# Mixture-of-experts FFN: transposes of h by VectorE squares and quadrant transfers, down projection two blocks behind, weight loads of experts 1 to 7 issued by GpSimd

## Chip, core and metric

One core of one Trainium2 chip runs the kernel. The metric is the device time in microseconds of one execution, as the median of repeated runs. Beside it stands one profiled execution, from which every row in this document comes.

## What is computed

Tokens x are (4, 512, 256). A first layer adds a normalised and projected x together with a decayed running sum over context rows that is gathered by patch index. The second layer, which the change concerns, is a mixture of experts: 2,048 tokens, 8 experts, the two best per token, width 256 to 1024 to 256, all in float32.

```python
x = x + xattn(layernorm(x), ctx_2048, mask, W_in, b_in, g_res, g_init)
z = layernorm(x)
probs = softmax(z @ gate_w)
w, idx = top_k(probs, 2); w = w / w.sum(-1, keepdims=True)
out = 0
for i in range(8):
    wi = where(idx == i, w, 0).sum(-1)
    h = silu(z @ w1[i]) * (z @ w3[i])       # 256 -> 1024
    out = out + (h @ w2[i]) * wi[..., None] # 1024 -> 256
x = x + out
```

## The kernel before

**Front part.** For some 114 us the kernel computes the first layer, the router, and lists that sort the tokens by expert into blocks of 128 token slots. At most 39 blocks can occur; here there are 37. A table in SBUF holds one word for each block: its expert, the expert of the block before, and flags that say which part of the next expert's weights is to be prepared in this step (F_CHUNK, F_W2, F_W3) and whether a further expert's weights are to be loaded (F_LOAD). Every engine reads this word and walks over the blocks in its own loop (`over_steps`, L289), two blocks per turn of the loop. What orders the engines among each other is semaphores alone; each engine works its own instructions in the order written.

**Precision.** A matrix product in float32 is made of three passes in the fast format (`three`, L1308): each operand is split into a high part (a ScalarE copy into float32r) and a low part (a VectorE subtraction), and hi*hi, hi*lo and lo*hi are accumulated. This holds for the weights (`split_hi` L313, `split_lo` L318, 2,048 columns a chunk, three chunks per expert) and for each transposed activation (`xT`, `hT`).

**One block.** GpSimd gathers 128 rows of z from DRAM (`block_rows`, L473). TensorE transposes them (L1319), ScalarE and VectorE split the result into xT_hi and xT_lo. TensorE makes gate and linear part for 512 of the 1024 hidden columns at a time (`up`, L1322, 12 matmuls of 512 columns for each of two halves); ScalarE does silu (L612), VectorE the product with the linear part, hmul (L1091). TensorE transposes hmul, four squares of 128x128 for each half (`hT`, L1331), into one PSUM bank per half. ScalarE copies it to hT_hi (L607), VectorE subtracts to get hT_lo (L1099). TensorE then does the down projection (`down`, L1338, 24 matmuls of 256 columns), ScalarE scales by the routing weight (`y`, L617) and GpSimd adds the rows to the output in DRAM by an indirect transfer (`add_rows`, L481), which waits until the add before it has landed.

**Order on TensorE in step i (L1353).** up half 0 of block i; transposes of h half 1 of block i-1; transposes of x of block i+1; up half 1; transposes of h half 0 of block i; down of block i-1. So the down projection is one block behind. `drain` (L1371) finishes the last block.

**Weights.** SyncE issues all of them (`raw_load`, L263: three transfers of 1 MB an expert; w1 and w3 have rows of 4 KB, w2 of 1 KB). Experts 0 and 1 are loaded in the front part, expert 2 once expert 0 is split, and expert e+3 in the step in which the last chunk of expert e+1 is split (L386 on). GpSimd splits the low parts of expert 0 itself (L461 to L471). In its steps SyncE does nothing else.

Of the kernel before, what the change touches and what calls it, by code (L numbers as in the profile page):

```python
# [22 lines left out]
P = 128  # L23
# [3 lines left out]
T = B * S  # L27
# [12 lines left out]
TABLE = 1 + 2 * STEP_PAIRS + 3  # L40
# [4 lines left out]
OUT_INIT = 32  # L45
# [6 lines left out]
def build(nc, x, ctx, lens, w_in, b_in, g_res, g_init, gate_w, w1, w3, w2, out):  # L52
# [12 lines left out]
    with stack:  # L65
# [111 lines left out]
        with ExitStack() as early:  # L177
# [9 lines left out]
        dg = sb("dg", [P, 2, TPB, D], f32)  # L187
# [59 lines left out]
            hT0hi_ready hT0lo_ready hT1hi_ready hT1lo_ready xT_done xThi_ready xTlo_ready  # L247
# [7 lines left out]
        blk_in = [sem(f"blk_in{q}") for q in range(2)]  # L255

# [32 lines left out]
        def over_steps(eng, body):  # L289

            body(0, 0, 0, step_word(eng, 0))
            with eng.Fori(0, STEP_PAIRS) as pair:
                word = step_word(eng, pair * 2 + 1)
                with eng.If(word & F_RUN):
                    body(pair * 2 + 1, 1, pair, word)
                    word = step_word(eng, pair * 2 + 2)
                    with eng.If(word & F_RUN):
                        body(pair * 2 + 2, 0, pair + 1, word)

        def block_count(eng):  # L300
            eng.wait_ge(s["blocks_ready"], 1)
            return eng.value_load(blocks_i[:, :], min_val=E, max_val=BLOCKS)

        def at_end(eng, blocks, drain):

            with eng.If(blocks & 1):
                drain(blocks - 1, 0)
            with eng.If((blocks + 1) & 1):
                drain(blocks - 1, 1)
# [17 lines left out]
        def _(sp):  # L327
# [31 lines left out]
            parts = [(e, m) for e in range(2) for m in range(3)]  # L359
            for k in range(B + 2):  # L360
# [17 lines left out]
                for e, m in parts[max(k - 1, 0):k] if k < B + 1 else parts[k - 1:]:  # L378
                    raw_load(sp, e, e, s["raw_ready"] if e else s["raw_first"], (m,))


            sp.wait_ge(s["lo_first"], 3)
            sp.wait_ge(s["raw_ready"], RAW_SEM)
            sp.wait_ge(s["xT_done"], 1)
            raw_load(sp, 2, 0, s["raw_ready"])
            sp.wait_ge(s["table_ready"], 1)  # L386

            def step(i, q, half, word):
                with sp.If(word & F_LOAD):
                    e = expert(word).with_bounds(min_val=0, max_val=E - 4)  # L390
                    sp.wait_ge(s["lo_ready"], e * 3 + 6)
                    settle(sp)
                    sp.wait_ge(s["raw_ready"], RAW_SEM * (e + 2))
                    settle(sp)
# [1008 lines left out]
```

## Time and profile before

| | us |
|---|---|
| median of 3 runs | 495.22 |
| fastest run | 494.84 |
| span of the profiled execution (first to last instruction) | 492.8 |
| TensorE busy in it | 422.1 |
| VectorE busy | 263.6 |
| ScalarE busy | 192.5 |
| GpSimd busy | 169.9 |

Busy time is the time in which the engine works on at least one instruction; matmuls overlap each other and the weight loads (PEld), so a busy TensorE may still be able to be fuller. PEclk or granted clock is the share of TensorE's full 2.4 GHz that it was given; 0.5 is 1.2 GHz. SyncE (SP) has no compute; its rows are the issues of transfers, and "to landing" is the time from an issue to the completion of its data. The name behind "<-" in brackets is what ended the idle time before an instruction.

### The profile page before, as it was taken

What the parts mean: (1) busy time and instruction counts of PE and PEld (TensorE: products, weight loads), DVE (VectorE), ACT (ScalarE), POOL (GpSimd) and SP (SyncE); (2) the same over time, 40 slices, a digit from 0 to 9 for tenths busy, and PEclk for the clock granted to TensorE, in tenths of its full rate; (3) what the DMA queues carried; (4) which work ended last, traced back from release to release, by engine and by line L of the source; (5) the groups of instructions that cost most, each with busy time, mean ns of one, the idle gap of its engine ahead of it and who ended that gap; (6) DMA issues with size and microseconds to landing.
All of it is one profiled execution on the core that took longest, in us unless ns stands there. A gap on an engine that the chain in (4) does not pass through costs nothing.

```text
span 492.8 us, 10407 instructions
## 1 busy us (share of the span) xinstructions
PE 422.1 (86%) x2557; PEld 365.9 (74%) x2558; DVE 263.6 (53%) x670; ACT 192.5 (39%) x334; POOL 169.9 (34%) x133
## 2 busy tenths in 40 slices
PE   0678984314999999999999999999999999999980
PEld 0556864313888889888888988888898888889870
DVE  7877869997454255433563564355356433653230
ACT  3446443301444246233542643354264334542230
POOL 5455434442023333322242333224233322532321
PEclk9979795555999999999999999999999999999995
DMA  6856885604415421541118118111811211121120
GB/s 196 297 179 206 272 268 157 200 1 139 161 23 160 149 32 32 203 105 23 30 21 287 32 21 283 32 26 21 287 32 21 32 30 23 21 32 32 21 32 11
DMA packets 33076, 50.92 MB, mean 103 GB/s; under 512 B 3335, under 2 KB 25095, under 8 KB 33063
## 3 DMA queue, kind: packets, MB, share of 16 engines
q1 hardware_dynamic: 24983, 38.44, 23.4%
q0 software_dynamic: 8080, 12.33, 12.8%
q8 instruction: 5, 0.08, 0.1%
q14 instruction: 8, 0.07, 0.0%
HBM read 39.36 MB, written 11.40 MB: 103 GB/s over the span
## 4 chain that ended last, share of the span: by engine, by line
PE 73%; DVE 7%; issue 2%; DMA 1%; POOL 1%; ACT 1%; ACTq 0%; POOLq 0%; DVEq 0%
PE bank L1312 64%; PE bank L1335 7%; PE bank L1319 2%; DVE ctx_sb L901 2%; DVE onehot_lo L986 1%; DVE rank L889 1%; DMA dg<-depool_rows,plugi 1%; PE bank L1266 1%; POOL dg L441 1%; DMA xblk<-z_rows,gidx 1%; PE bank L1191 0%; DVE batch L990 0%; POOL out L485 0%; DVE st L823 0%; DVE x_all L820 0%
## 5 line engine op out<-in xcount | busy, mean ns | idle before, releaser
L1312 PE MATMUL bank<-split,xT_hi 128*128 x592 | 166.8, 403 | 1.3 <-DVE xT_lo L1087 1.3
L1096 DVE TENSOR_TENSOR hmul<-gact,bank 128x512 f32<-128x512 f32 x74 | 50.9, 688 | 149.1 <-ACT gact L614 149.1
L485 POOL DMA_INDIRECT out<-yblk,itok x37 | 78.4, 2118 | 149.8 <-ACT yblk L621 138.2
L1312 PEld LDWEIGHTS bank<-split,xT_hi 128*128 128x128 f32 x592 | 106.9, 190 | 22.6 <-issue 1.9
L1312 PE MATMUL bank<-split,hT 128*128 (+1 forms) x888 | 115.4, 286 | 1.4 <-issue 0.8
L1312 PEld LDWEIGHTS bank<-split,hT 128*128 128x128 f32 x888 | 108.5, 191 | 2.1 <-issue 1.2
L614 ACT ACTIVATE gact<-bank 128x512 f32<-128x512 f32 x74 | 44.2, 598 | 158.9 <-PE bank L1312 158.8
L1312 PE MATMUL bank<-split,xT_lo 128*128 x296 | 93.7, 398 | 0.0
L477 POOL DMA_INDIRECT xblk<-z_rows,gidx x40 | 40.1, 1001 | 106.0 <-DVE gidx L1109 100.3
L321 DVE TENSOR_TENSOR split<-raw,split x21 | 48.1, 2293 | 37.6 <-ACT split L315 37.6
L1312 PEld LDWEIGHTS bank<-split,xT_lo 128*128 128x128 f32 x296 | 56.0, 189 | 13.5
L1102 DVE TENSOR_TENSOR hT<-bank,hT 128x512 fp32r<-128x512 f32 x74 | 50.6, 684 | 3.7 <-ACT hT L609 3.7
L315 ACT ACTIVATE split<-raw (+1 forms) x24 | 45.9, 1912 | 2.8 <-issue 1.9
L1335 PEld LDWEIGHTS bank<-ident,hmul 128*128 128x128 f32 x296 | 36.9, 141 | 10.3 <-DVE hmul L1096 0.4
L1335 PE MATMUL bank<-ident,hmul 128*128 128x128 f32 x296 | 44.4, 272 | 0.0
L609 ACT ACTIVATE hT<-bank 128x512 fp32r<-128x512 f32 x74 | 43.9, 593 | 1.1 <-issue 1.0
L621 ACT ACTIVATE yblk<-bank,wtok 128x256 f32<-128x256 f32 x37 | 17.6, 475 | 47.5 <-PE bank L1312 35.7
L605 ACT ACTIVATE xT_hi<-bank 128x256 fp32r<-128x256 f32 x38 | 14.9, 392 | 21.2 <-PE bank L1319 21.2
L441 POOL DMA_INDIRECT dg<-depool_rows,plugi x16 | 15.5, 969 | 19.7 <-issue 12.1
L1087 DVE TENSOR_TENSOR xT_lo<-bank,xT_hi 128x256 fp32r<-128x256 f32 x38 | 15.8, 415 | 3.2 <-ACT xT_hi L605 3.2
L1245 PE MATMUL bank<-gate,batch 128*128 128x8 f32 x64 | 11.5, 317 | 6.8 <-DVE base L880 6.1
L1245 PEld LDWEIGHTS bank<-gate,batch 128*128 128x128 f32 x64 | 11.1, 270 | 7.6 <-DVE base L880 6.5
(182 smaller groups left out, 332.4 us busy)
## 6 DMA issues: line engine op xcount, KB each, us to landing
raw<-in_L_ffn_w SPq DMA_DIRECT2D x24, 1024.0 KB, 8.0
ctx_sb<-in_ctx SPq DMA_DIRECT2D x4, 1024.0 KB, 6.4
x_all<-in_x SPq DMA_DIRECT2D x4, 512.0 KB, 8.3
depool_rows<-gact SPq DMA_DIRECT2D x4, 512.0 KB, 3.0
out<-x_all SPq DMA_DIRECT2D x4, 512.0 KB, 5.5
z_rows<-z SPq DMA_DIRECT2D x4, 512.0 KB, 3.9
xblk<-z_rows,gidx POOLq DMA_INDIRECT x40, 2.8
out<-yblk,itok POOLq DMA_INDIRECT x37, 4.7
```

The costliest lines, as they stand in the source:

```text
L315: act.activation(split_chunk[:, ds(raw3 * 2 + m, 1)], raw_chunk[:, ds(raw3 + m, 1)], ACT.Copy)\
L321: dve.tensor_tensor(split_chunk[:, ds(raw3 * 2 + m + 3, 1)], raw_chunk[:, ds(raw3 + m, 1)], split_chunk[:, ds(raw3 * 2 + m, 1)].bitcast(f3 ...
L441: pool.indirect_dma_start(dg[:, b % 2, j, :], None, depool_dram[b][:, :], bass.IndirectOffsetOnAxis(ap=plugi[:, n:n + 1], axis=0))\
L477: pool.indirect_dma_start(xblk[:, q, :], None, z_dram[:, :], bass.IndirectOffsetOnAxis(ap=gidx[:, q:q + 1], axis=0))\
L485: pool.indirect_dma_start(out[:, :], bass.IndirectOffsetOnAxis(ap=itok[:, q:q + 1], axis=0), yblk[:, q, :], None, compute_op=ALU.add).then ...
L609: act.activation(hT_hi[:, q, half * KF // 2:(half + 1) * KF // 2], p_hT[half][:, :], ACT.Copy)\
L614: act.activation(gact[:, half * HALF:(half + 1) * HALF], p_gate[half][:, :], ACT.Silu)\
L1096: dve.tensor_tensor(hmul[:, cols], gact[:, cols], p_lin[part][:, :], ALU.mult)\
L1102: dve.tensor_tensor(hT_lo[:, q, ks].rearrange("p k t -> p (k t)"), p_hT[part][:, :], hT_hi[:, q, ks].bitcast(f32).rearrange("p k t -> p (k ...
L1245: mm = pe.matmul(p_logit[:, j * E:(j + 1) * E], zT[:, j, k * P:(k + 1) * P], gate[:, k, :], start=(k == 0), stop=(k == KD - 1))
L1312: mm = pe.matmul(out_, xp, w_, start=start and n == 0, stop=stop and n == 2)
L1335: mm = pe.transpose(p_hT[part][:, k * P:(k + 1) * P], hmul[:, f0:f0 + P], ident[:, :])
```

## The change

1. **Transposes.** TensorE no longer transposes h, but for the last block. VectorE transposes the 32x32 squares inside each group of 32 partitions (a quadrant), one instruction of 128x512 for each half of h (`turn`), into the new tile swap_in. SyncE then moves the squares between quadrants in 16 transfers from swap_in to swap_out (`exchange`: for each source quadrant a and target quadrant b 32 partitions with 1 KB each). ScalarE makes hT_hi of all 1024 columns out of swap_out in one instruction, and VectorE hT_lo in one, both with permuted access. swap_in and swap_out have two buffers each, by the parity of the block, and take the place in SBUF of the tile dg of the front part.
2. **Order.** The down projection is of block i-2 in step i. ScalarE's hT(i-1) comes after its second silu of step i and waits there for the 16 transfers; y(i-2) comes behind it, ahead of the weight split. VectorE's hT(i-1) comes after both turns. `over_steps` has two blocks ahead of its loop, `drain` finishes two blocks: the transposes of the last by TensorE, then both downs. The table word's field for the expert before means two blocks before.
3. **Weight loads.** GpSimd issues those of experts 1 to 7: expert 1 ahead of its split of expert 0, expert 2 before the steps, the others in the step, behind the gather and the add. SyncE keeps expert 0 and in its steps only has exchanges.
4. Three transfers pad the output instead of two.

```diff
+            def exchange(i, q):
+                sp.wait_ge(s["swap_ready"], 2 * (i + 1))
+                settle(sp)
+                if after(i, 2):
+                    sp.wait_ge(s["hTlo_ready"], i - 1)
+                    settle(sp)
+                for a in range(NQ):
+                    for b in range(NQ):
+                        sp.dma_start(swap_out[b * Q:(b + 1) * Q, q, a], swap_in[a * Q:(a + 1) * Q, q, b])\
+                          .then_inc(swapped[q], 16)
...
+            raw_load(pool, 1, 1, s["raw_ready"])
             split_lo(pool, 0, 0, 0, "lo_first")
...
+            pool.wait_ge(s["lo_first"], 3)
+            pool.wait_ge(s["raw_ready"], RAW_SEM)
+            settle(pool)
+            raw_load(pool, 2, 0, s["raw_ready"])
+
+            def step(i, q, half, word):
                 pool.wait_ge(s["xT_done"], i + 2)
                 block_rows(i + 3, 1 - q)
-                if not isinstance(i, int):
-                    add_rows(i - 1, 1 - q)
+                if after(i, 2):
+                    add_rows(i - 2, q)
+                with pool.If(word & F_LOAD):
+                    e = expert(word).with_bounds(min_val=0, max_val=E - 4)
+                    pool.wait_ge(s["lo_ready"], e * 3 + 6)
+                    settle(pool)
+                    pool.wait_ge(s["raw_ready"], RAW_SEM * (e + 2))
+                    settle(pool)
+                    raw_load(pool, e + 3, (e + 1) & 1, s["raw_ready"])
...
             def hT(i, q, half):
-                act.wait_ge(s[f"th{half}_done"], i + 1)
-                act.activation(hT_hi[:, q, half * KF // 2:(half + 1) * KF // 2], p_hT[half][:, :], ACT.Copy)\
-                   .then_inc(s[f"hT{half}hi_ready"], 1)
+                act.wait_ge(swapped[q], EXCHANGE * half)
+                act.activation(hT_hi[:, q].rearrange("p k (a t) -> p a k t", a=NQ), swap_out[:, q], ACT.Copy)\
+                   .then_inc(s["hThi_ready"], 1)
...
                 silu(i, 0)
-                if later:
-                    hT(i - 1, 1 - q, 1)
                 xT(i + 1, 1 - q)
                 silu(i, 1)
-                hT(i, q, 0)
+                if after(i, 1):
+                    hT(i - 1, 1 - q, half + q)
+                if after(i, 2):
+                    y(i - 2, q)
...
+            def turn(i, q, half, part):
+                dve.wait_ge(s[f"h{part}_done"], i + 1)
+                if after(i, 2):
+                    dve.wait_ge(swapped[q], EXCHANGE * half)
                 ks = slice(part * KF // 2, (part + 1) * KF // 2)
+                dve.transpose(swap_in[:, q, :, ks, :].rearrange("p b k t -> p k b t"),
+                              hmul[:, part * HALF:(part + 1) * HALF].rearrange("p (k b t) -> p k b t", b=NQ, t=Q))\
+                   .then_inc(s["swap_ready"], 1)
...
                 h(i, 0)
-                if later:
-                    hT(i - 1, 1 - q, 1)
-                    meta(i - 1, 1 - q)
                 xT(i + 1, 1 - q)
+                turn(i, q, half, 0)
                 next_index(i + 3, 1 - q, half + q + 1)
                 h(i, 1)
-                hT(i, q, 0)
+                turn(i, q, half, 1)
+                if after(i, 1):
+                    hT(i - 1, 1 - q)
+                if after(i, 2):
+                    meta(i - 2, q)
...
             def step(i, q, half, word):
                 slot = word & 1
                 pe.wait_ge(s["xTlo_ready"], i + 1)
                 pe.wait_ge(s["lo_ready"], expert(word) * 3 + 2)
+                if after(i, 1):
+                    pe.wait_ge(s["h0_done"], i)
 
                 up(slot, q, 0)
-                if later:
-                    hT(i - 1, 1)
                 xT(i + 1, 1 - q, half + q)
 
+                if after(i, 1):
+                    pe.wait_ge(s["h1_done"], i)
                 up(slot, q, 1)
-                hT(i, 0)
-                if later:
-                    down(i - 1, 1 - q, expert_before(word), (word >> PREV_BIT) & 1)
+                if after(i, 2):
+                    down(i - 2, q, expert_before(word), (word >> PREV_BIT) & 1, s["hTlo_ready"], i - 1)
```

## Rows read from the trace of the kernel before

**Rows 1.** Page, part 1: busy us (share of the span) xinstructions of each engine.

```profile
PE 422.1 (86%) x2557; PEld 365.9 (74%) x2558; DVE 263.6 (53%) x670; ACT 192.5 (39%) x334; POOL 169.9 (34%) x133
```

**Rows 2.** List of waits: waiter <- waited for: us in total, times, longest us.

```profile
ACT gact L614 <- PE bank L1312: 158.8, 73, 4.4
```

**Rows 3.** Timeline of one step: start us, length us, engine, line, out<-in, count.

```profile
302.58 1.09 PE L1312 MATMUL bank<-split,xT_hi 128*128 x4
...
305.38 0.60 PE L1335 MATMUL bank<-ident,hmul 128*128 128x128 f32 x4
...
305.82 0.38 PE L1319 MATMUL bank<-ident,xblk 128*128 128x128 f32 x2
...
308.84 0.60 PE L1335 MATMUL bank<-ident,hmul 128*128 128x128 f32 x4
...
309.20 3.11 PE L1312 MATMUL bank<-split,hT 128*128 x24
...
312.14 1.09 PE L1312 MATMUL bank<-split,xT_hi 128*128 x4
```

**Rows 4.** Window: us, busy (x) of PE, PEld, DVE, ACT, POOL, clock; the transposes.

```profile
172.36:468.72 296.36, 296.36 (x1800) 259.58 (x1799) 137.08 (x266) 125.11 (x205) 98.16 (x62) 1.00 0.28 70
...
L1335 PE MATMUL bank<-ident,hmul 128*128 128x128 f32 x248 | 37.1, 272 | 0.0
```

**Rows 5.** Groups by form, 172.36 to 468.72: count, busy us, mean ns, idle before.

```profile
L1096 DVE TENSOR_TENSOR hmul<-gact,bank 128x512 f32<-128x512 f32 x62 | 42.7, 688 | 127.2 <-ACT gact L614 127.2
L1102 DVE TENSOR_TENSOR hT<-bank,hT 128x512 fp32r<-128x512 f32 x62 | 42.4, 684 | 0.0
L321 DVE TENSOR_TENSOR split<-raw,split x18 | 41.3, 2293 | 32.1 <-ACT split L315 32.1
L609 ACT ACTIVATE hT<-bank 128x512 fp32r<-128x512 f32 x63 | 37.3, 593 | 0.0
...
L315 ACT ACTIVATE split<-raw x18 | 34.5, 1914 | 2.2 <-issue 1.6
```

**Rows 6.** Timeline of SyncE's issues, opening burst and two later ones.

```profile
2.81 0.42 SPq L340 DMA_DIRECT2D x_all<-in_x  x1
...
7.89 4.07 SPq L340 DMA_DIRECT2D x_all<-in_x  x2
...
61.07 0.37 SPq L376 DMA_DIRECT2D z_rows<-z  x1
61.48 0.71 SPq L267 DMA_DIRECT2D raw<-in_L_ffn_w  x1
```

**Rows 7.** Queue totals, issues with median us to landing, and landings of the gathers (L477).

```profile
q1 hardware_dynamic: 24983, 38.44, 23.4%
...
raw<-in_L_ffn_w SPq DMA_DIRECT2D x24, 1024.0 KB, 8.0
...
depool_rows<-gact SPq DMA_DIRECT2D x4, 512.0 KB, 3.0
...
out<-yblk,itok POOLq DMA_INDIRECT x37, 4.7
...
DMA to landing us min/median/max: 2.7/2.8/6.5
```

**Rows 8.** GpSimd's issues, ns min/median/max, first and last start, and one split.

```profile
L426 POOL DMA_DIRECT2D out<-zeros x2: 567/684/801, 16.6 to 17.4; - x2
...
L477 POOL DMA_INDIRECT xblk<-z_rows,gidx x40: 940/991/1467, 114.0 to 471.4; - x40
...
L485 POOL DMA_INDIRECT out<-yblk,itok x37: 1579/2522/2857, 141.6 to 481.3; - x37
...
88.16 4.93 POOL L321 TENSOR_TENSOR split<-raw,split 128x2048 fp32r<-128x2048 f32 x1 [5.82 <-ACT split L315]
```

**Rows 9.** Timeline: block 0's second product, and the last down's second half.

```profile
129.65 0.69 DVE L1096 TENSOR_TENSOR hmul<-gact,bank 128x512 f32<-128x512 f32 x1 [1.96 <-ACT gact L614]
...
477.89 1.70 PE L1312 MATMUL bank<-split,hT 128*128 128x256 f32 x12 [0.65 <-DVE hT L1102]
```

More of the change, by code:

```diff
@@ L255, in build @@
         blk_in = [sem(f"blk_in{q}") for q in range(2)]
+        swapped = [sem(f"swapped{q}") for q in range(2)]
         block = stack.enter_context(nc.Block())
@@ L289, in over_steps, with after, blocks_less_two, at_end @@
         def over_steps(eng, body):
-            body(0, 0, 0, step_word(eng, 0))
+            for i in range(2):
+                body(i, i, 0, step_word(eng, i))
             with eng.Fori(0, STEP_PAIRS) as pair:
-                word = step_word(eng, pair * 2 + 1)
+                word = step_word(eng, pair * 2 + 2)
                 with eng.If(word & F_RUN):
-                    body(pair * 2 + 1, 1, pair, word)
-                    word = step_word(eng, pair * 2 + 2)
+                    body(pair * 2 + 2, 0, pair + 1, word)
+                    word = step_word(eng, pair * 2 + 3)
                     with eng.If(word & F_RUN):
-                        body(pair * 2 + 2, 0, pair + 1, word)
-        def block_count(eng):
+                        body(pair * 2 + 3, 1, pair + 1, word)
+        def after(i, n):
+            return not isinstance(i, int) or i >= n
+        def blocks_less_two(eng):
             eng.wait_ge(s["blocks_ready"], 1)
[L302 to L309, printed above, removed]
+            return eng.value_load(blocks_i[:, :], min_val=E - 2, max_val=BLOCKS - 2)
+        def at_end(eng, less_two, drain):
+            with eng.If(less_two & 1):
+                drain(less_two + 1, 0)
+            with eng.If((less_two + 1) & 1):
+                drain(less_two + 1, 1)
         def split_hi(act, raw3, m):
@@ L377, in _ @@
                       .then_inc(z_out[b], 16)
[L378 to L385, printed above, removed]
-            sp.wait_ge(s["table_ready"], 1)
-            def step(i, q, half, word):
[L389 to L394, printed above, removed]
-                    raw_load(sp, e + 3, (e + 1) & 1, s["raw_ready"])
+                for e, m in parts[max(k - 1, 0):k]:
+                    raw_load(sp, e, e, s["raw_first"], (m,))
+            sp.wait_ge(s["table_ready"], 1)
+            def exchange(i, q):
[8 more added lines that the diff above has]
+                          .then_inc(swapped[q], 16)
+            def step(i, q, half, word):
+                exchange(i, q)
+            less_two = blocks_less_two(sp)
             over_steps(sp, step)
+            for q in range(2):
+                sp.wait_ge(swapped[q], ((less_two + 3 - q) >> 1) * EXCHANGE)
+                settle(sp)
         @block.gpsimd
@@ L493, in _ @@
             block_rows(1, 1)
-            blocks = block_count(pool)
+            less_two = blocks_less_two(pool)
             pool.wait_ge(s["table_ready"], 1)
@@ L1150, in drain @@
             def drain(i, q):
-                hT(i, q, 1)
+                hT_last(i, q, 0)
+                hT_last(i, q, 1)
+                meta(i - 1, 1 - q)
                 meta(i, q)
-            blocks = block_count(dve)
+            less_two = blocks_less_two(dve)
             over_steps(dve, step)
-            at_end(dve, blocks, drain)
+            at_end(dve, less_two, drain)
         @block.tensor
@@ L1353, in step @@
             def step(i, q, half, word):
-                later = not isinstance(i, int) or i > 0
                 slot = word & 1
```

107 lines of the change are left out of this document (57 added, 50 removed).

## Prediction

> **What bounds the kernel now.** I began with the busy shares. TensorE is busy 422.1 of 492.8 us, the next engine 263.6 [rows 1]. The list of waits shows that the others wait for it: ScalarE's silu alone stood 158.8 us behind matmuls [rows 2]. So I took one block's step from the timeline [rows 3]. It begins at 302.58 with the first up projection (12 matmuls, 2.80 us). Four transposes of h follow at 305.38, the second up projection from 305.96, four transposes at 308.84, 24 down matmuls at 309.20, and the next step at 312.14: 9.56 us with no idle TensorE time. From 172.36 to 468.72, 31 such steps, TensorE is busy for all 296.36 us at the full 2.4 GHz clock (1.00), and the transposes number 248, eight a step [rows 4]. VectorE is busy 137.08 us of that window, 4.42 a step; ScalarE 4.04; GpSimd 3.17. Each saved TensorE microsecond is therefore a saved microsecond, until one of these, or a transfer, takes a step's time.
>
> **Transposes off TensorE.** The chain from 305.38 to the two transposes of x is 0.44 us for four, and 308.84 to 309.20 is 0.36 for the other four [rows 3]. So eight cost 0.80 to 0.88, depending on whether the switch between kinds of matmul stays; I take the middle, 0.84. Of 37 blocks only the last keeps them (drain): 36 x 0.84 = 30.2 us. The step becomes 8.72.
>
> **VectorE.** Per step it loses two reads of 684 ns (hT_lo) and gains two transposes of 128x512 and one subtraction of 128x1024, SBUF to SBUF [rows 5]. The subtraction lies between the 512-column row (684) and the 2048-column row (2293, the split): a line through both gives 1.22 us. No row shows a VectorE transpose. The nearest is the 512-column product, 688 ns; I take that, with twice it, 1.38, as the upper bound for four-byte elements and half of it, 0.34, as the lower; the lower changes no sum. VectorE: 4.42 - 1.37 + 1.38 + 1.22 = 5.65 a step on average (7.03 at the bound), and about 6.6 in a step with a split (8.0 at the bound), all below 8.72. ScalarE trades two reads of 593 for one of 1024 columns, 1.03 us by the line from 593 to 1914: 0.16 less.
>
> **The exchange.** SyncE now issues 16 transfers per block, each 32 rows of 1 KB. A spaced issue takes 0.37 us and the next begins 0.41 after it [rows 6]: 16 x 0.41 = 6.6 us, about 6.9 with the waits. In the opening burst ten issues from 2.81 to 7.89 are 0.56 apart, and the last two took 4.07 together with the queue full [rows 6]. I take 0.41, since each exchange transfer leaves only two rows per DMA engine queued, far from that backlog. The bytes are small: 512 rows a step are 32 per engine, at 74 ns per packet (23.4% of 16 x 492.8 us over 24,983 packets) 2.4 us per step [rows 7]. A write out of SBUF of 512 KB lands 3.0 us after its issue, of which 2.4 are its bytes at that rate [rows 7]; a single 32 KB transfer lands between 0.7 and 3.0 after its own. I take 1.9, the middle. So swap_ready to swapped is 15 x 0.41 + 1.9 = 8.1 us.
>
> Is it covered? Counting from a step's start: the second up ends at 5.8, silu (0.6), product and transpose (0.69 each) with 0.1 to 0.2 between engines end at 8.2, the exchange at 16.3. ScalarE reaches hT in the next step after its second silu, at 8.72 + 6.6 = 15.3, so it waits 1.0 us, but y behind it waits for down's end at 17.4 anyway. With 1.03 and 1.22, hT_lo is ready at 18.7; TensorE asks for it at 17.4 + 5.8 = 23.2. Slack 4.5 us. Queued behind that wait on ScalarE are y, the split (1.91) and the next silu: 16.3 + 1.1, y until 17.9, split until 19.9, silu due 20.5. It fits. On VectorE, the split_lo behind it ends at about 22.2 against a product due at 21.1, which slides, and TensorE needs that product only at 26.2. The down's place, two blocks behind, pays for all this.
>
> Rule and row differ on one thing. Ten transfers were issued 0.56 apart and the three of a weight load, issued within 1.6 us, land a median 8.0 after issue [rows 6, 7], so transfers in one queue overlap. The Trainium skill (DMA: Bandwidth & Descriptors, Anatomy of one DMA, and Rules for kernel authors) gives a fixed 2.0 us per transfer, calls those under 64 KB mostly overhead and says that transfers to disjoint partition groups serialize. Taken in series its figures would make an exchange an estimated 33 us.
>
> **Weight loads on GpSimd.** Seven experts' loads (21 transfers of 1 MB) leave SyncE's queue. Issuing 64 rows took GpSimd 0.57 to 0.80 us, gathering 128 rows 0.99 [rows 8]. A load has 256 + 256 + 1024 rows. Lower bound: 3 x 0.57 = 1.7 us. Upper, by rows: 1536 x 0.99 / 128 = 11.9. I take 4, nearer the direct issue, whose two transfers differ by start-up rather than by rows. Behind it in the same queue stand the next gather and add. The load starts after the step's last split, at about 13.6. Its bytes take 8 us (its landing, 8.0 [rows 7]), so the next gather lands at about 13.6 + 4 + 8 + 2.8 = 28.4; TensorE wants that block three steps on, at 26.2 + 2.8 = 29.0. At the upper bound it lands 1 to 3 us late. In the other direction, a gather that runs beside a load lands after 6.5 us instead of 2.8 [rows 7]: with that delay the exchange takes 11.8 us of the 12.6 that are free. I charge 0.2 us per load, six loads: 1.2; bounds 0 and 18 (3 us each). Expert 1's load, ahead of GpSimd's first split at 77.8, has a 5.8 us idle gap behind that split [rows 8]; nothing.
>
> **Head and end.** The first steps have no down to hide the latency. Block 0's second product ends at 130.34 [rows 9], the exchange at 139.2, ScalarE's hT, a split of 1.91 and silu of step 2 then run to 142.8, and TensorE reaches step 3 at about 145.6 where its work alone would allow 143.3: 2.3 us lost against 1.0 lost there before: +1.3. At the end the transposes and the waits for them (0.65 us before 477.89 by its row, and as much again before the first of their kind) hide under a down: -1.3. But y of the last two blocks is now only 2.9 us apart, and the last add waits until the one before has landed (4.7 us [rows 7]): +1.9. All other edits (table one longer, three padding transfers, done_before) move nanoseconds or hide in idle GpSimd time.
>
> **Sum.** -30.2 + 1.2 + 1.3 - 1.3 + 1.9 = -27.1 us. The profiled span of 492.8 goes to 465.7; the median of the runs is 2.4 above the span, so 495.2 - 27.1 = 468.1.
>
> **Rivals.**
> - *A, the exchange sets the step but still gains.* At the opening burst's 0.56 per issue SyncE needs 16 x 0.56 + 0.3 = 9.3 us a step. 36 x (9.56 - 9.3) = 9 us gained, 3 lost at head and end: 489. Transposes at 1.38 instead lengthen the loop from one exchange to the one after next (8.1 + 1.1 + 1.2 + VectorE's next products and transposes, and a ScalarE and VectorE split in 21 of 37 steps) to some 18.0 us per two steps instead of 17.4: 36 x 0.3 = 11 us, 479. For it: the spacing row. Against: the 0.41 rows.
> - *B, slower.* The same place, SyncE's issue of small SBUF-to-SBUF transfers, decides from (9.56 - 0.3) / 16 = 0.58 us per transfer. At 0.66 the step is 10.9 and the kernel 495 + 36 x 1.3 = 542; at the full queue's 2.0 each it would be over 1300. Nothing shows such a transfer, so it can't be excluded. By the skill's rule above (its 2.0 us in series) B would hold; the overlap in the rows speaks against it.
> - *C, weight loads late.* GpSimd's long issue, lengthened by VectorE, holds up gathers: 6 x 3 us, 486. For it: the add takes from 1.58 to 2.86 us, median 2.52 [rows 8], and 21 of 37 steps have a VectorE split that it can meet; the new subtraction has two SBUF inputs as the split has, 1.22 us in every step. Against: the gathers held to 0.99. The Trainium skill (SBUF — State Buffer, the physically separate sides) says that such a VectorE operation and a GpSimd operation lock each other out of a shared port, and advises the hardware queues for loads; the trace's spread of the add agrees. It names no price for this case.
>
> **Chances.** Forecast, TensorE-bound at 8.7: 0.60 (461 to 475: 0.88 saved per step and no head or load cost give 461; 1 us per load and the head doubled give 475). A 0.13 (475 to 495), C 0.10 (475 to 488), B 0.14, the change not taking effect 0.03 (495). Range 460 to 495: it leaves out B, and half of the last. A measurement here tells about 2% from no change, that is 485 to 505. Faster by more: 0.60 + half of A + most of C = 0.76; within: 0.10; slower: 0.14.
>
> **What would show it.** TensorE's chain with steps of 8.7 us and no transposes of h before the last block; SyncE issues of 0.41 in trains of 6.6 us; a VectorE transpose near 0.69; ScalarE's wait for the exchange about 1 us; GpSimd's direct issues 1 to 2 us each; x gathers landing late only beside loads. I am wrong if TensorE idles each step for hT_lo or h0_done (A, B), or only after loads, for xblk (C), or if the transposes cost more than they took.

## The result

The changed kernel takes 574.36 us (median of 4 runs, 572.94 to 576.13) against 495.03 for the kernel before: ratio 1.162, 95% interval 1.159 to 1.166. One of the four runs of the kernel before, at 1086.1 us, is left out of the ratio. The prediction was 468.1, range 460 to 495. It was wrong; it had named a slower kernel as its rival B, at 0.14.

The page of the changed kernel, parts 1 and 4 (the chain of work that ended last, by engine and by line):

```profile
PE 424.8 (74%) x2269; PEld 353.9 (62%) x2270; DVE 310.8 (54%) x708; ACT 189.8 (33%) x298; POOL 168.9 (30%) x155
...
SPq 55%; issue 14%; DVE 12%; PE 6%; DMA 5%; POOL 3%; ACT 2%; DVEq 2%; POOLq 0%; ACTq 0%
SPq L405 52%; DMA swap_out<-swap_in 2%; PE bank L1368 2%; SPq L281 2%; POOL dg L458 1%; DVE ctx_sb L938 1%; DVE rank_lo L928 1%; DVE onehot_lo L1023 1%; DVE hmul L1131 1%; ACT hT L638 1%; PE bank L1261 1%; DMA dg<-depool_rows,plugi 1%; DVE onehot_lo L785 1%; DVE swap_in L1140 1%; DMA out<-yblk,itok 1%
```

TensorE was the engine to follow before [rows 1]. Now it has 6% of the chain, and one line of SyncE's queue, the exchange's issues, has 52%. TensorE's granted clock, 1.00 from 172.36 to 468.72 us in the kernel before [rows 4], is 0.96 in the same stretch now, in which TensorE is busy for 245.96 us of 296.36. The transposes are gone (2,269 matmuls, 288 fewer), yet the other engines wait: the list of waits, longest in total, begins

```profile
ACT hT L638 <- DMA swap_out<-swap_in: 199.7, 36, 8.4
...
DVE hT L1147 <- ACT hT L638: 115.7, 34, 6.2
...
ACT yblk L657 <- DVE itok L1169: 51.8, 35, 1.6
```

where the list before began with ScalarE waiting for matmuls [rows 2]. ScalarE waited for each of 36 exchanges, 5.5 us on average. SyncE's timeline (start, length, count), the first block's exchange, and the longest stretch without any wait late in the kernel, when no weight load is left:

```profile
134.61 10.13 SPq L405 DMA_DIRECT2D swap_out<-swap_in  x16
...
398.70 101.69 SPq L405 DMA_DIRECT2D swap_out<-swap_in  x142
```

Sixteen issues take 10.13 us, (10.13 - 0.59) / 15 = 0.636 apart; 0.59 is the median length of one. The 142 in 101.69 are 0.716 apart on average, 11.46 us for a block: 10.2 of issues and 1.3 between two blocks' issues, where SyncE's code has its waits, the table word and the loop (what each of these costs was not measured). In the kernel before, issues stood 0.41 apart [rows 6]. The remaining terms of the sum are in the groups of the page and GpSimd's timeline:

```profile
L1147 DVE TENSOR_TENSOR hT<-swap_out,hT 128x1024 fp32r<-128x1024 f32 x36 | 44.1, 1224 | 115.7 <-ACT hT L638 115.7
L638 ACT ACTIVATE hT<-swap_out 128x1024 fp32r<-128x1024 f32 x36 | 38.1, 1060 | 199.7 <-DMA swap_out<-swap_in 199.7
...
L1140 DVE STREAM_TRANSPOSE swap_in<-hmul 128x512 f32<-128x512 f32 x74 | 52.3, 706 | 1.3
...
77.93 2.49 POOL L274 DMA_DIRECT2D raw<-in_L_ffn_w  x3
```

### The profile page after: what moved, and what is told of

Its sections match the earlier page's. It is cut to its first block, busy times and chain, and to the rows that moved or that the text cites. A ratio compares the mean times of both kernels' runs of the same rounds, so it can differ in the third digit from the quotient of the medians.

```text
span 572.4 us, 10753 instructions
## 1 busy us (share of the span) xinstructions
PE 424.8 (74%) x2269; PEld 353.9 (62%) x2270; DVE 310.8 (54%) x708; ACT 189.8 (33%) x298; POOL 168.9 (30%) x155
## 4 chain that ended last, share of the span: by engine, by line
SPq 55%; issue 14%; DVE 12%; PE 6%; DMA 5%; POOL 3%; ACT 2%; DVEq 2%; POOLq 0%; ACTq 0%
SPq L405 52%; DMA swap_out<-swap_in 2%; PE bank L1368 2%; SPq L281 2%; POOL dg L458 1%; DVE ctx_sb L938 1%; DVE rank_lo L928 1%; DVE onehot_lo L1023 1%; DVE hmul L1131 1%; ACT hT L638 1%; PE bank L1261 1%; DMA dg<-depool_rows,plugi 1%; DVE onehot_lo L785 1%; DVE swap_in L1140 1%; DMA out<-yblk,itok 1%
## 5 line engine op out<-in xcount | busy, mean ns | idle before, releaser
L1368 PE MATMUL bank<-split,xT_hi 128*128 x592 | 180.3, 429 | 45.3 <-DVE xT_lo L1124 40.5
L1368 PEld LDWEIGHTS bank<-split,xT_hi 128*128 128x128 f32 x592 | 114.4, 203 | 74.3 <-issue 51.9
L1368 PE MATMUL bank<-split,hT 128*128 (+1 forms) x888 | 119.3, 292 | 33.4 <-ACT yblk L657 29.5
L1368 PEld LDWEIGHTS bank<-split,hT 128*128 128x128 f32 x888 | 114.1, 198 | 44.5 <-issue 42.3
L503 POOL DMA_INDIRECT out<-yblk,itok x37 | 59.0, 1595 | 194.8 <-issue 102.7
L1147 DVE TENSOR_TENSOR hT<-swap_out,hT 128x1024 fp32r<-128x1024 f32 x36 | 44.1, 1224 | 115.7 <-ACT hT L638 115.7
L638 ACT ACTIVATE hT<-swap_out 128x1024 fp32r<-128x1024 f32 x36 | 38.1, 1060 | 199.7 <-DMA swap_out<-swap_in 199.7
L1368 PE MATMUL bank<-split,xT_lo 128*128 x296 | 99.3, 418 | 0.0
L495 POOL DMA_INDIRECT xblk<-z_rows,gidx x40 | 40.4, 1010 | 126.8 <-DVE gidx L1162 116.2
L650 ACT ACTIVATE gact<-bank 128x512 f32<-128x512 f32 x74 | 44.0, 594 | 27.3 <-PE bank L1368 16.6
L1140 DVE STREAM_TRANSPOSE swap_in<-hmul 128x512 f32<-128x512 f32 x74 | 52.3, 706 | 1.3
L274 POOL DMA_DIRECT2D raw<-in_L_ffn_w x21 | 17.1, 829 | 19.1 <-issue 19.1
L458 POOL DMA_INDIRECT dg<-depool_rows,plugi x16 | 15.9, 993 | 19.5 <-issue 12.7
L1301 PE MATMUL bank<-gate,batch 128*128 128x8 f32 x64 | 12.7, 336 | 6.3 <-DVE base L917 5.9
```

What stands on the lines that cost most here:

```text
L495: pool.indirect_dma_start(xblk[:, q, :], None, z_dram[:, :], bass.IndirectOffsetOnAxis(ap=gidx[:, q:q + 1], axis=0))\
L503: pool.indirect_dma_start(out[:, :], bass.IndirectOffsetOnAxis(ap=itok[:, q:q + 1], axis=0), yblk[:, q, :], None, compute_op=ALU.add).then ...
L638: act.activation(hT_hi[:, q].rearrange("p k (a t) -> p a k t", a=NQ), swap_out[:, q], ACT.Copy)\
L650: act.activation(gact[:, half * HALF:(half + 1) * HALF], p_gate[half][:, :], ACT.Silu)\
L1140: dve.transpose(swap_in[:, q, :, ks, :].rearrange("p b k t -> p k b t"), hmul[:, part * HALF:(part + 1) * HALF].rearrange("p (k b t) -> p ...
L1147: dve.tensor_tensor(hT_lo[:, q].rearrange("p k (a t) -> p a k t", a=NQ), swap_out[:, q], hT_hi[:, q].bitcast(f32).rearrange("p k (a t) -> ...
```

## The experiments

Three theories stood against each other at first. Theory 1: the time SyncE needs to issue is the whole loss. Theory 2: the latency from the last issue through hT_hi, hT_lo and what follows on ScalarE and VectorE is what counts. Theory 3 was that weight loads on GpSimd's queue hold up the rest. In the table, each ratio is to runs of the kernel before made beside that run (their medians were 494.0 to 494.6). n12 and its variant leave out a quarter of h, n8 and its variants half of it, and `forms` feeds the down projection wrong data; the others compute everything.

| run | exchange | order of splits | us | ratio, 95% interval |
|---|---|---|---|---|
| changed kernel | 16 | as changed | 574.4 | 1.162 (1.159 to 1.166) |
| n12 | 12 | as changed | 519.0 | 1.050 (1.048 to 1.053) |
| n8 | 8 | as changed | 492.4 | 0.996 (0.995 to 0.997) |
| n8_meta | 8 | meta first | 469.5 | 0.949 (0.947 to 0.951) |
| n8_order | 8 | split and meta first | 464.3 | 0.939 (0.937 to 0.942) |
| n12_order | 12 | split and meta first | 486.9 | 0.985 (0.983 to 0.987) |
| order16 | 16 | split and meta first | 569.5 | 1.152 (1.149 to 1.156) |
| bounce | 5, over DRAM | as changed | 522.9 | 1.058 (1.054 to 1.061) |
| bounce_order | 5, over DRAM | split and meta first | 477.8 | 0.966 (0.964 to 0.968) |
| bounce_order_spread | the same, loads in thirds | split and meta first | 490.8 | 0.990 (0.985 to 0.995) |
| bounce_order_sp | the same, loads by SyncE | split and meta first | 497.4 | 1.006 (1.005 to 1.008) |
| loads_alone | none, TensorE's transposes | as before the change | 493.8 | 0.999 (0.998 to 1.000) |
| forms | 16, four of each of four forms | as changed | 553.1 (one run) | none |

### Fewer transfers: n12 and n8

```diff
                     for b in range(NQ):
+                        if a != b:
                             sp.dma_start(swap_out[b * Q:(b + 1) * Q, q, a], swap_in[a * Q:(a + 1) * Q, q, b])\
```

(n8 has `if (a + b) % 2:` in its place.)

> The changed kernel with 12 of the 16 exchange transfers: the four with equal source and target quadrant are left out, and swap_out is set to zero once, so a quarter of h is missing in the down projection of all blocks but the last. Theory 1, SyncE's time to issue sets the step: in the changed kernel 16 issues stand 0.635 us apart and a block takes 11.54 us, of which 16 x 0.635 = 10.2 are issues and 1.3 the gap between two blocks' issues. With 12 it is 12 x 0.635 + 1.3 = 8.9 us per block, just over TensorE's 8.72, and the kernel takes 574 - 37 x 4 x 0.635 = 480 us. Theory 2, the latency from the last issue through landing, hT_hi, hT_lo and the product (the loop over two blocks) sets it: four issues less shorten the loop by 2.5 us per two blocks, 574 - 18 x 2.5 = 529. Theory 3, the weight loads on GpSimd's queue hold up the rest: no more than 20 us gained.

> The changed kernel with 8 of the 16 exchange transfers (those whose quadrants' numbers add up to an odd number), swap_out set to zero once, so half of h is missing in the down projection of all blocks but the last. Theory 1: SyncE needs 8 x 0.635 + 1.3 = 6.4 us, TensorE becomes the bound at 8.7 a block, and the time is about 466 to 470, as the prediction's sum has it. It should be 10 us or so below the kernel with 12, not another 94. If the time falls by 94 again, TensorE was not where I put it. Theory 2 (latency loop): 529 - 45 = 484. Theory 3 (loads): TensorE idles after each of six loads, above 480.

n12 took 519.0 and n8 492.4. Theory 1 wanted 480 and 466 to 470, theory 2 529 and 484, so neither fits alone; n12's gain is also far more than the 20 us that theory 3 left room for. Four transfers less gave 55 us, then only 27. In n8 SyncE is no longer busy, for it waits for VectorE's squares:

```profile
SPq L294 <- DVE swap_in L1141: 123.1, 35, 14.4
```

(19.0 us in 5 waits in the changed kernel), and still the kernel is no faster than the one before the change. So a second cost lay behind the first. The list of waits of n8 names it:

```profile
ACT yblk L658 <- DVE itok L1170: 90.3, 35, 4.9
...
ACT hT L639 <- DMA swap_out<-swap_in: 55.6, 26, 6.0
```

ScalarE's y waits for meta_ready; VectorE's two copies of meta stand behind hT_lo, and hT_lo stands behind ScalarE's hT_hi. Behind y on ScalarE stands the split, behind which stands VectorE's split, behind which stands the next product. The timeline of the changed kernel shows the whole chain in one piece, in one of the 21 of 37 steps that have a split:

```profile
306.93 1.06 ACT L638 ACTIVATE hT<-swap_out 128x1024 fp32r<-128x1024 f32 x1 [6.24 <-DMA swap_out<-swap_in]
...
308.02 1.22 DVE L1147 TENSOR_TENSOR hT<-swap_out,hT 128x1024 fp32r<-128x1024 f32 x1 [5.05 <-ACT hT L638]
...
309.23 0.14 DVE L1169 COPY itok<-idx_all 128x1 int32 x1
309.46 0.47 ACT L657 ACTIVATE yblk<-bank,wtok 128x256 f32<-128x256 f32 x1 [1.47 <-DVE itok L1169]
310.21 1.92 ACT L327 ACTIVATE split<-raw  x1 [0.27 <-issue]
...
312.71 2.29 DVE L333 TENSOR_TENSOR split<-raw,split  x1 [3.34 <-issue]
...
314.92 0.68 DVE L1131 TENSOR_TENSOR hmul<-gact,bank 128x512 f32<-128x512 f32 x1
...
317.21 0.71 DVE L1140 STREAM_TRANSPOSE swap_in<-hmul 128x512 f32<-128x512 f32 x1
```

From the landed exchange at 306.9 to the end of the second transpose at 317.9 it is 11.0 us, and only then can the exchange of the block after next begin. An exchange of 8 transfers takes 8 x 0.635 and some 2 us of landing (the changed kernel's first begins at 134.6, and ScalarE's hT_hi behind it at 146.0). By this estimate that is 18 us over two blocks, where two TensorE-bound steps take 17.4; with 12 it is 20.6, enough to put n12 above theory 1, and with 16 it is 23, as much as SyncE's two times 11.46.

### The chain broken: n8_order, n8_meta and order16

```diff
                 silu(i, 1)
-                if after(i, 1):
-                    hT(i - 1, 1 - q, half + q)
-                if after(i, 2):
-                    y(i - 2, q)
...
                 with act.If(word & F_CHUNK):
...
                     split_hi(act, raw3, chunk_of(word))
+                if after(i, 1):
+                    hT(i - 1, 1 - q, half + q)
+                if after(i, 2):
+                    y(i - 2, q)
...
                 turn(i, q, half, 1)
-                if after(i, 1):
-                    hT(i - 1, 1 - q)
                 if after(i, 2):
                     meta(i - 2, q)
...
                     split_lo(dve, e + 1, raw3, chunk_of(word))
+                if after(i, 1):
+                    hT(i - 1, 1 - q)
```

n8_meta changes one thing of it: VectorE's meta stands ahead of hT_lo, and the splits stay behind.

> The kernel with 8 transfers (h is half left out, as there), and one thing more: ScalarE's and VectorE's first weight split of a step moved ahead of hT_hi and hT_lo, and VectorE's meta ahead of them too. In the kernel with 8 transfers steps with a split take 9.8 us and others 8.7: ScalarE waits for the transfers, does hT_hi, waits for VectorE's hT_lo and the two copies of meta, does y, then the split, and VectorE's split and the next product follow one after the other. Theory 2b, this chain over ScalarE and VectorE set the 9.8: now the splits lie in the time of the exchange, all steps fall to 8.7 but those beside a weight load, and the kernel takes 492 - 21 x 1.1 = 469. Theory 3, only the weight loads cost (steps of 13.7): 490. If the split steps stay at 9.8 for another reason: 492.

> Which part of the reordering gave the 28 us between the kernel with 8 transfers (492.4) and the same with the order changed (464.3)? Here only VectorE's meta moves ahead of hT_lo, the splits stay behind; half of h is left out as there. If y's wait for meta behind hT_lo was the cost, ScalarE gets its y 1.2 us and the two copies' time sooner in every step: that is 1.5 us less in each chain over two blocks with a split, 21 x 0.75 = 16 us or more, 477 or below. If it is the splits behind the wait, 488 to 492.

> The changed kernel, whole computation, with the same reordering of the splits, 16 transfers. Theory 1, SyncE issues in 16 x 0.635 + 0.65 to 1.3 = 10.8 to 11.5 us per block and nothing else counts: 560 to 574, no or hardly any gain, and SyncE never waits for swap_ready. Theory 2b, the chain and the issues were both in series (11.5 us of issues and landing, 11 us of ScalarE and VectorE over two blocks): the chain falls to some 17 per two blocks, SyncE alone is left, 556. The two are told apart by SyncE's waits in the changed kernel (19 us) which would go to zero.

n8_order took 464.3, 28 us below n8 and 4.7 below the 469 expected. The rows of x's transposes (two a step; count, first and last start) of n8, n8_meta and n8_order, in this order, from 184 to 262 us:

```profile
L1377 PE MATMUL bank<-ident,xblk x16: 270/272/329, 190.3 to 255.3; 128*128 128x128 f32 x16
```

```profile
L1377 PE MATMUL bank<-ident,xblk x18: 270/272/273, 187.2 to 256.9; 128*128 128x128 f32 x18
```

```profile
L1382 PE MATMUL bank<-ident,xblk x18: 270/272/273, 184.9 to 254.5; 128*128 128x128 f32 x18
```

Taking off the 0.1 us between the two of a step, n8 needs 64.9 / 7 = 9.27 us a step, n8_meta and n8_order 69.6 / 8 = 8.70 and 69.5 / 8 = 8.69. The prediction's 8.72 for a step bound by TensorE is met, also in a stretch with splits and a weight load. Meta alone gave 22.9 of the 28.1 us, so y's wait for it was the larger part, and the place of the splits the last 5.2.

order16, with the same order and 16 transfers, took 569.5, only 4.9 below the changed kernel. So with 16 transfers SyncE's issues are the bound, as theory 1 has it, and the chain costs next to nothing on top. SyncE's only wait for VectorE's squares is 13.2 us in one wait, that for the first block:

```profile
SPq L294 <- DVE swap_in L1142: 13.2, 1, 13.2
```

### Twelve with the new order: n12_order

> 12 of the 16 transfers (the same quarter of h left out as in the kernel with 12) and the splits ahead of hT. SyncE's law: 0.635 a transfer plus what lies between two blocks' issues. The reordered kernel with 16 ends in steps of 11.2 to 11.4, so the rest is 1.1 and with 12 it is 12 x 0.635 + 1.1 = 8.7, exactly TensorE's 8.7: steps of 8.7 to 8.9, 464 to 472, with somewhat longer ones after loads, since SyncE cannot catch up. If the time is far above (over 480), the latency of the exchange and not the issue is what is left.

486.9, above the expected 464 to 472 and above the 480 from which the expectation put it down to the exchange's latency. SyncE's timeline shows 37 issues in a stretch without a wait:

```profile
424.88 27.51 SPq L406 DMA_DIRECT2D swap_out<-swap_in  x37
```

27.51 / 37 x 12 = 8.9 us a block, as 12 x 0.635 + 1.3 has it. In a late stretch without loads (429.2 to 455.4) TensorE nevertheless makes steps of 8.7. The long steps stand beside the weight loads: one of 16.0 us beside the first load in the steps, some 11 us for each of four others, 16 us in sum of the 22.6 between this kernel and n8_order. At the first, GpSimd issues the load at 154.9, the block's 12 issues begin from 151.6 to 159.5, and hT_hi begins at 165.8:

```profile
165.82 1.06 ACT L639 ACTIVATE hT<-swap_out 128x1024 fp32r<-128x1024 f32 x1 [10.03 <-DMA swap_out<-swap_in]
```

From the last issue's start to hT_hi it is 6.3 us; it was 1.9 for the changed kernel's first exchange, which has no load beside it. In n8_order, with SyncE at 6.4 a block, the same loads leave only one step of 9.3. That SyncE's lack of slack at 8.9 is what makes the difference is the likely reading; it was not tried by itself.

### What an issue costs: forms

```diff
-                for a in range(NQ):
-                    for b in range(NQ):
-                        sp.dma_start(swap_out[b * Q:(b + 1) * Q, q, a], swap_in[a * Q:(a + 1) * Q, q, b])
+                for b in range(NQ):
+                    sp.dma_start(swap_out[b * Q:(b + 1) * Q, q, 0], swap_in[0:Q, q, b])
+                for b in range(NQ):
+                    ks = slice(b * 2, b * 2 + 2)
+                    sp.dma_start(swap_out[:, q, 1, ks], swap_in[:, q, 1, ks])
+                for b in range(NQ):
+                    sp.dma_start(side[q, b], swap_in[2 * Q:3 * Q, q, b].rearrange("p k t -> p (k t)"))
+                for b in range(NQ):
+                    sp.dma_start(swap_out[b * Q:(b + 1) * Q, q, 3].rearrange("p k t -> p (k t)"), z_dram[b * Q:(b + 1) * Q, :])
```

> What makes an issue take 0.59 us instead of 0.37? The 16 transfers of a block are replaced by four of each of four forms: SBUF to SBUF with 32 rows of 1 KB (as in the changed kernel), SBUF to SBUF with 128 rows of 256 bytes, SBUF to DRAM with 32 rows of 1 KB, DRAM to SBUF with 32 rows of 1 KB; the down projection gets a wrong h by this. If the number of rows decides, the 128-row form takes 0.37 and the three others 0.59. If it is SBUF on both sides, the first two take 0.59 and the last two 0.37. If it is neither but the issue one after the other without a pause, all take 0.59.

The semaphore increments are left out of the cut above. `side` is a DRAM tensor. The four forms' issues, in this order, ns min/median/max:

```profile
L405 SPq DMA_DIRECT2D swap_out<-swap_in x148: 573/590/1482, 134.8 to 529.1; - x148
```

```profile
L409 SPq DMA_DIRECT2D swap_out<-swap_in x148: 592/601/772, 138.3 to 531.7; - x148
```

```profile
L412 SPq DMA_DIRECT2D side<-swap_in x148: 407/424/632, 140.9 to 533.9; - x148
```

```profile
L415 SPq DMA_DIRECT2D swap_out<-z_rows x148: 311/422/602, 142.9 to 535.8; - x148
```

The number of rows does not decide: 128 rows take 0.60 and 32 rows 0.59. What decides is that both sides are SBUF. With DRAM on either side it is 0.42. The first two forms are also written with access patterns of one dimension more than the last two; that does not explain it, for the reads from DRAM in bounce, below, have more dimensions still and take 0.43. (Why it is so was not tried; a 128-row write to DRAM in the kernel before took 0.37 [rows 6].)

### Around the issues: bounce and bounce_order

```diff
-                for a in range(NQ):
-                    for b in range(NQ):
-                        sp.dma_start(swap_out[b * Q:(b + 1) * Q, q, a], swap_in[a * Q:(a + 1) * Q, q, b])
+                sp.dma_start(bounce[q].rearrange("p b k t -> p (b k t)"), swap_in[:, q].rearrange("p b k t -> p (b k t)"))\
+                  .then_inc(bounced[q], 16)
+                sp.wait_ge(bounced[q], 16 * (half + 1))
+                settle(sp)
+                for b in range(NQ):
+                    sp.dma_start(swap_out[b * Q:(b + 1) * Q, q],
+                                 bounce[q, :, b].rearrange("(a p) k t -> p a k t", a=NQ))\
+                      .then_inc(swapped[q], 16)
```

`bounce` is a DRAM tensor; the write has 128 rows of 4 KB.

> A way around SyncE's issues, with the whole computation kept: VectorE's squares go to DRAM in one transfer of 128 rows of 4 KB, SyncE waits for it, and four transfers, one for each target quadrant of 32 rows with four pieces of 1 KB, bring them back. 5 issues instead of 16. By theory 1 SyncE is busy 5 x 0.6 + 3.0 for the landing (as the 512 KB write out of SBUF in the kernel before) + 1.3 = 7.3 us a block, below 8.72, and swap_ready to swapped is about 0.4 + 3.0 + 4 x 0.635 + 2.5 = 8.4 us, near the 8.1 of the prediction: the time is about 468, faster than both. By theory 2 the latency is what counts; 8.4 is close to the changed kernel's 15 x 0.635 + 2 = 11.5 less 3: some 520. By theory 3 nothing changes but the loads' part: above 480.

> The exchange over DRAM with 5 transfers, whole computation, and the splits reordered. Without the order it took 522.9: SyncE idle, swap_ready to swapped about 9.2 us (write landing 3.5, reads 3.2, issues), steps beside weight loads 14 to 15.8. Theory 2b: the loop over two blocks is now 9.2 + 1.1 + 1.2 + 3.2 us of products and transposes, 15 in all, below 17.4, so steps without a load are 8.7; six steps beside a load stay 5 us long. 466 + 6 x 5 = 496. Theory 3 alone (loads): 515.

bounce took 522.9, where theory 1 alone had 468 and theory 2 some 520: SyncE waits for VectorE's squares 109.2 us in 29 waits and for its own write to land 139.2 us in 36, and the chain remains, with an exchange of some 9 us. bounce_order, the same with the new order, took 477.8: 3.4% below the kernel before the change and 16.8% below the changed one. It computes everything and is the version to keep. The expectation was 496; the steps beside loads cost less than I charged. The two forms' issues in bounce_order, and its transposes of x from 141.7 to 182.2 us (four steps from the first pair to the fifth, one load issued at 152.4):

```profile
L405 SPq DMA_DIRECT2D bounce<-swap_in x37: 15/342/499, 134.0 to 456.7; - x37
```

```profile
L410 SPq DMA_DIRECT2D swap_out<-bounce x148: 302/431/812, 138.5 to 460.7; - x148
```

```profile
L1386 PE MATMUL bank<-ident,xblk x10: 270/272/273, 141.7 to 182.2; 128*128 128x128 f32 x10
```

40.4 / 4 = 10.1 us a step there, and from 364.3 to 416.6, after the last load, 52.2 / 6 = 8.7. Five steps beside loads take 10.5 to 13.1 us, 12.7 above five of 8.7. So nearly all of the distance to n8_order's 464.3 lies beside the loads.

### The loads: loads_alone, bounce_order_sp, bounce_order_spread

> The kernel before with the third part of the change alone: GpSimd issues the weight loads of experts 1 to 7, TensorE transposes h as before. My prediction charged 0.2 us a load and bounded it at 3. By the theory that loads matter only through the exchange beside them nothing here waits for them: 494 to 496, no difference. By the rival (gathers and adds behind a load in GpSimd's queue come late) there are steps longer than 9.56 after each load: 500 to 512.

```diff
-                    raw_load(sp, e + 3, (e + 1) & 1, s["raw_ready"])
+                    raw_load(pool, e + 3, (e + 1) & 1, s["raw_ready"])
```

(in the kernel before, and likewise for experts 1 and 2.) 493.8 against 494.0, ratio 0.999 (0.998 to 1.000): the third part of the change costs nothing in sum, and its steps take 9.56 as before.

The traces show that this sum hides two differences. The prediction gave expert 1's load in the front part no cost. Yet the first transposes of x start at 119.7 us in the changed kernel and in loads_alone, against 117.1 in the kernel before. GpSimd issues this load in front of its first split, and one VectorE instruction that begins beside them ends only with the split. First the kernel before, then the changed one:

```profile
77.82 4.51 POOL L321 TENSOR_TENSOR split<-raw,split 128x2048 fp32r<-128x2048 f32 x1
78.05 4.31 DVE L889 CAST rank<-blk 128x8 int32<-128x8 f32 x1
```

```profile
77.93 2.49 POOL L274 DMA_DIRECT2D raw<-in_L_ffn_w  x3
78.37 6.61 DVE L928 TENSOR_SCALAR rank_lo<-rank 128x8 int32<-128x8 int32 x1
80.39 4.55 POOL L333 TENSOR_TENSOR split<-raw,split 128x2048 fp32r<-128x2048 f32 x1
84.89 0.16 DVE L930 TENSOR_SCALAR rank_hi<-rank 128x8 int32<-128x8 int32 x1
```

The next instruction, of the same kind and size, takes 0.16 us; this one took 6.61, and the one held up in the kernel before 4.31. The difference, 2.3 us, is nearly all of the head's 2.6. At the other end, loads_alone ends 8.2 us after the start of its last add, the kernel before 11.5; why was not tried.

> The exchange over DRAM with the order of splits changed, and the third part of the change undone: SyncE issues all weight loads again, in the same queue as the exchange, behind the exchange of the same step. Theory: each DMA engine works one queue's entries in order, so the next exchange stands behind 3 MB, 8 us, and the five or six steps beside a load grow from 10.5 to 13 (loads on GpSimd's queue) to 14 to 17: 490 to 500 instead of 477.8. Rival: the engines are full either way and the queue does not matter: 478. Second rival: GpSimd's issues were the cost there, and SyncE's are cheaper: 465 to 472.

With SyncE issuing the loads again 497.4, 19.7 us worse than bounce_order and within the 490 to 500 that the theory gave. One load and the exchange behind it are shown next, first in bounce_order_sp, where both are in SyncE's queue:

```profile
199.96 1.62 SPq L276 DMA_DIRECT2D raw<-in_L_ffn_w  x3
203.34 3.52 SPq L409 DMA_DIRECT2D bounce<-swap_in  x1
216.36 1.77 SPq L414 DMA_DIRECT2D swap_out<-bounce  x4
```

then in bounce_order, where GpSimd issued the load from 200.60 to 203.37:

```profile
205.21 0.07 SPq L405 DMA_DIRECT2D bounce<-swap_in  x1
213.48 1.73 SPq L410 DMA_DIRECT2D swap_out<-bounce  x4
```

From the write's issue to the first read's it is 13.0 us behind the load in one queue, and 8.3 beside the load in two; without a load it is 2.7 (254.45 to 257.17 in bounce_order_sp). The issue itself took 3.52 us instead of 0.34. The five long steps are 14.0 to 16.4 us in bounce_order_sp, 10.5 to 13.1 in bounce_order, 18.7 more in sum. So the loads are better on GpSimd's queue when SyncE has this exchange. For the exchange of 16 transfers this was not tried.

> As the kernel before in this list, but GpSimd loads each third (1 MB) of an expert's weights in the step in which that third's place has been split, so that a load is 2.7 us of the DMA engines in three steps instead of 8 in one. Theory 3, a load's 3 MB in one go hold up the exchange past the free time: the steps of 14 us go, and the time is 468 to 472, 5% below the kernel before the change. If the steps stay long in sum (the delay depends on the bytes, not on how they are bunched), 490 to 496.

```diff
-                    raw_load(pool, e + 3, (e + 1) & 1, s["raw_ready"])
+                    for n, here in enumerate(((m + 3) & 2, m & 1, m & 2)):
+                        with pool.If(here):
...
+                            raw_load(pool, e + 3, (e + 1) & 1, s["raw_ready"], (n,))
...
-            dve.tensor_tensor(f_load, two_, low4, ALU.mult).then_inc(s["fields_ready"], 1)
+            dve.tensor_tensor(f_load, f_chunk, low4, ALU.mult).then_inc(s["fields_ready"], 1)
```

490.8 (484.9 to 492.4) instead of 477.8: thirds are worse, against the expectation of 468 to 472; it is the other case of the expectation, 490 to 496. The long steps do not go away: there are five of them again, 11.7 to 16.6 us instead of 10.5 to 13.1. In the longest, ScalarE waits for the reads of the exchange:

```profile
358.42 1.06 ACT L655 ACTIVATE hT<-swap_out 128x1024 fp32r<-128x1024 f32 x1 [10.44 <-DMA swap_out<-bounce]
```

Why one exchange per expert lands so late although each load is a third was not tried; this stays open.

## Why the prediction was wrong

**Step of 8.72, transposes 0.84 us a block: right.** n8_order shows 8.69 a step, and its 464.3 lies 3.8 below the forecast: head, end and loads together cost less there than the 3.1 charged. (The lower edge of the forecast's band does not come out of its own terms: 495.2 - 36 x 0.88 - 1.3 + 1.9 is 464.1, not 461. Nothing rests on it.)

**VectorE and ScalarE's new work: right.** 706 ns for a transpose (688 taken), 1224 for hT_lo (1.22) and 1060 for hT_hi (1.03).

**Issue on SyncE: the step that failed, a term that was mis-sized.** The prediction took 16 x 0.41 = 6.6 us and 0.3 for the rest. Measured: 16 x 0.636 = 10.2 and 1.3. The sum is 11.46 instead of 6.9, above TensorE's 8.7. The 0.41 came from transfers with DRAM on one side; no row showed one between SBUF and SBUF, and the unknown was bounded from above by 0.56 of the opening burst, not by what lay beyond it. Against 9.56 before, (11.46 - 9.56) x 37 = 70 us, of the 79 lost; 2.6 more are the longer head, and the rest was not taken apart. The prediction's threshold for this rival, 0.58 a transfer, was right in kind and too high in number: with 1.3 of rest it is (9.56 - 1.3) / 16 = 0.52. A fifth of the error of 4.6 us is in that rest, which was never read from a row.

**Cover of the exchange: a second step that failed.** The prediction listed what stands behind ScalarE's wait, y among it, and let y wait for down's end alone. It waits for meta too, and the change moved meta behind hT_lo. That joins two engines into one chain of 11 us. By the prediction's own times hT_lo is ready at 18.7, so y begins at about 19 and not at 17.4. The prediction also asked only when TensorE needs VectorE's late product, and not when the exchange behind that product begins; its loop from one exchange to the one after next stands under rival A, for slow transposes alone. With 16 transfers it hides behind SyncE (order16: 4.9 us); with 8 it costs 28.1 us. The assumed price of an issue would not have saved the forecast: n8's exchange, some 7 us, is shorter than the 8.1 that the prediction assumed, and n8 took 492.4, about as long as the kernel before.

**Latency in series.** The Trainium skill (DMA: Bandwidth & Descriptors, Anatomy of one DMA) gives a fixed cost per transfer, measured there for transfers issued by GpSimd, that taken in series would make an exchange an estimated 33 us. In the changed kernel it took 11.4 from the first issue to hT_hi (134.6 to 146.0), so transfers did overlap, and B did not come about by that rule. The Trainium skill (DMA: Bandwidth & Descriptors, Rules for kernel authors) says that transfers under 64 KB are mostly overhead. The trace agrees, in the issue: 0.59 us for 32 KB whose bytes, two rows per DMA engine at 74 ns [rows 7], are 0.15.

**Loads on GpSimd: right that they cost little,** by wrong sizes: three issues took 2.49 us, not 4, and a load of 1024 rows took 0.95 against 0.77 for one of 256. Expert 1's load, put at nothing, cost the head 2.6 us, since a VectorE instruction was held up beside it. Rival C did not occur alone (loads_alone, 0.999).

C's argument from the add can be read from the traces. In the kernel before, 17 of 37 adds, beside which VectorE has no split, take 1.58 or 1.59 us; 19 lie beside a split for 1.05 to 1.38 us and take 2.52 to 2.86, about as much longer; one lies beside it for 0.2 and takes 1.75. In the changed kernel no add lies beside a split or beside the new subtraction, and all take 1.55 to 1.68:

```profile
L503 POOL DMA_INDIRECT out<-yblk,itok x37: 1552/1585/1677, 161.6 to 564.2; - x37
```

So this cost arises only where the two engines' instructions fall together, and the change moved the adds away from the splits.

## What to carry to other kernels

Count the instructions that a transfer's issuing engine executes per step, and take the price of an issue from a transfer with the same two memories on its sides; where no row has one, let the range reach to where it would decide. When a wait is moved, follow every semaphore that the instructions behind it wait for, on both engines: a small copy that was moved along, meta here, can chain two engines together. If a load moves to GpSimd, look at what VectorE does beside its issue. If an exchange between partitions is needed, one transfer out to DRAM and four back, with the waiting engine's own work put ahead of the wait, was 3.4% faster than the transposes on TensorE.

## What the runs showed of the hardware

An issue on SyncE took 0.59 to 0.60 us where both sides are SBUF, with 32 rows as with 128; 0.42 to 0.43 where one side is DRAM and the other has 32 rows; 0.34 for one write of 128 rows of 4 KB to DRAM. Between the issues of two blocks lay another 1.3 us. An issue behind a 3 MB load in the same queue took 3.52 us instead of 0.34, and its data 13.0 us until the reads behind them could be issued, against 8.3 with the load in GpSimd's queue and 2.7 without one. A 1 MB load issued by GpSimd took 0.77 us of GpSimd's time with 256 rows of 4 KB and 0.95 with 1024 rows of 1 KB. A VectorE transpose of 128x512 float32 in squares of 32x32 took 0.706 us, as much as an elementwise product of that size (0.69). A VectorE instruction of 128x8 elements that takes 0.16 us took 6.61 beside a load issue (2.49) and a split (4.55) on GpSimd. An add on GpSimd took 1.59 us alone and 2.5 to 2.9 where it lay 1.05 to 1.38 us beside a VectorE split.
